# Results of a mixture-of-experts stage: stored by slot and gathered back, or scattered to their tokens and loaded plainly

## What is computed

```python
gate_weights = jax.nn.softmax(gate_logits, axis=-1)
topk_w, topk_idx = jax.lax.top_k(gate_weights, TOP_K)            # TOP_K = 2 of 8 experts
...
for e in range(NUM_EXPERTS):
    gate = jax.nn.silu(jnp.einsum('bsd,dh->bsh', x, W1[e]))
    val = jnp.einsum('bsd,dh->bsh', x, W3[e])
    y = jnp.einsum('bsh,hd->bsd', gate * val, W2[e])
    out = out + combine[..., e:e + 1] * y
```

## Time and profile before

| | |
|---|---|
| median of 3 runs | 1237.82 us (1235.93 to 1239.07) |
| the profiled execution, its own time | 1233.52 us |
| its span | 1231.8 us |
| mean granted clock of TensorE | 0.933 |
| PE busy | 1066.2 us, 87% |
| DVE busy | 586.4 us, 48% |
| ACT busy | 365.1 us, 30% |
| POOL busy | 238.2 us, 19% |
| layer 1, the loop over tiles | about 151 to 219.5 us |
| layer 1, from the last result to X | 219.5 to 246.3 us |
| layer 5, the loop over tiles | about 669 to 866.6 us |
| layer 5, from the last result to X | 866.6 to 892.0 us |

### The profile page before, as it was taken

One profiled execution on the slowest core, in us unless ns is written; L12 is line 12 of the kernel. 1 busy time (PEld: TensorE's weight loads), 2 busy tenths in 40 slices (PEclk: granted clock), 3 DMA queues, 4 the chain that ended last, 5 costly groups with the idle time before them and its releaser, 6 DMA issues.

```text
span 1231.8 us, 17738 instructions
## 1 busy us (share of the span) xinstructions
PE 1066.2 (87%) x6818; PEld 739.2 (60%) x6818; DVE 586.4 (48%) x1320; ACT 365.1 (30%) x675; POOL 238.2 (19%) x317
## 2 busy tenths in 40 slices
PE   5877999979999999978774999999179999879989
PEld 4665578736766666667563777777045555443457
DVE  6976322345434343445474221122256676248592
ACT  3642123232122222214220121121004544425570
POOL 4212332520000000003521110100541322011350
PEclk9986999979999999999986999999659999978999
DMA  9002022201011010055043112110230000020000
GB/s 274 15 2 94 18 84 79 86 26 35 22 30 35 18 35 5 10 202 219 2 167 107 31 31 81 35 30 14 77 142 2 1 2 1 1 69 1 0 9 26
DMA packets 36954, 65.31 MB, mean 53 GB/s; under 512 B 4456, under 2 KB 27848, under 8 KB 35464
## 3 DMA queue, kind: packets, MB, share of 16 engines
q1 hardware_dynamic: 26504, 47.91, 11.6%
q0 software_dynamic: 3744, 10.23, 3.1%
q10 hardware_dynamic: 6624, 6.03, 1.4%
HBM read 53.93 MB, written 10.22 MB: 52 GB/s over the span
## 4 chain that ended last, share of the span: by engine, by line
PE 73%; DVE 15%; issue 3%; DMA 3%; ACT 3%; POOL 2%; SPq 0%; DVEq 0%; ACTq 0%
PE bank L344 20%; PE bank L1132 12%; PE bank L1156 6%; PE bank L2020 5%; PE bank L1407 5%; PE bank L1415 2%; PE bank L2453 2%; PE bank L2064 2%; PE bank L2043 2%; PE bank L2035 2%; PE bank L1145 2%; PE bank L1392 1%; PE bank L1385 1%; PE bank L2075 1%; DVE big L1257 1%
## 5 line engine op out<-in xcount | busy, mean ns | idle before, releaser
L1132 PE MATMUL bank<-big 128*128 x552 | 153.8, 422 | 3.4 <-ACT big L1006 2.4
L344 PE MATMUL bank<-XNT,big 128*128 128x512 f32 x296 | 144.6, 641 | 4.5 <-DVE big L2202 2.8
L1132 PEld LDWEIGHTS bank<-big 128*128 128x128 f32 x552 | 96.4, 191 | 50.2 <-issue 11.9
L2020 PE MATMUL bank<-big,xs 32*128 32x512 f32 x256 | 85.7, 718 | 37.2 <-DVE xs L271 33.4
L265 POOL TENSOR_TENSOR rstd<-ve,half 128x1 f32<-128x1 f32 x64 | 38.8, 606 | 407.8 <-DVE ve L259 407.6
L1928 DVE TENSOR_REDUCE big<-bank 128x2 f32<-128x512 f32 x128 | 82.1, 685 | 49.9 <-PE bank L2020 49.8
L344 PEld LDWEIGHTS bank<-XNT,big 128*128 128x128 f32 x296 | 58.3, 204 | 73.0 <-issue 64.9
L1156 PE MATMUL bank<-big 128*128 (+1 forms) x368 | 87.2, 380 | 1.1 <-ACT big L1021 1.1
L1980 ACT ACTIVATE big<-bank 128x1024 f32<-128x1024 f32 x64 | 62.0, 1021 | 67.8 <-PE bank L2043 67.8
L950 DVE TENSOR_TENSOR big<-big,bank 128x704 f32<-128x704 f32 x23 | 20.4, 889 | 124.7 <-ACT big L1014 124.7
L344 PE MATMUL bank<-CTXT,big 128*128 128x512 f32 (+1 forms) x192 | 67.2, 494 | 10.7 <-DMA big<-wvT 10.7
(11 more groups left out here) (347 smaller groups left out, 1809.7 us busy)
## 6 DMA issues: line engine op xcount, KB each, us to landing
big<-m_gu SPq DMA_DIRECT2D x8, 1408.0 KB
big<-a_qkv SPq DMA_DIRECT2D x16, 384.0 KB, 3.6
big<-m_d SPq DMA_DIRECT2D x8, 768.0 KB
yg<-big ACTq DMA_DIRECT2D x46, 128.0 KB, 1.7
big<-m_gu SPq DMA_DIRECT2D x8, 352.0 KB
big<-a_o SPq DMA_DIRECT2D x16, 128.0 KB, 2.2
big<-p_gu SPq DMA_DIRECT2D x1, 2048.0 KB, 8.0
big<-m_d SPq DMA_DIRECT2D x8, 176.0 KB
```

The costliest lines, as they stand in the source:

```text
L344: ins = e.matmul(out, a, b, start=start and n == 0, stop=stop and n == len(pairs) - 1)
L1132: ins = e.matmul(out, xgT[s % 2][:, kb, :], WB[:, bass.ds(at[s] + (kb * 2 * F + c * chunk), chunk)], start=kb == 0, stop=kb == KB - 1)
L2020: e.matmul(bank[:, SBK + step % SBN, :], k.xs[t % 2][q, b * P:(b + 1) * P], cm[t % 2][q, 2 * jp:2 * jp + 2].rearrange("p j n -> p (j n)"), ...
```

## The change

The results no longer lie in `yg` by slot, but by token. `inv` now holds, for each slot, 128 + token + 1024*q, where q says whether it is the token's first or second expert; an empty slot still has 0. Rows 0 to 127 of `xn` and `yg` are there for the empty slots.

- **Stores of the normalised rows**: `xn` holds every row twice (at 128 + token and at 1152 + token), so that the same `inv` serves the fetch. SP stores each tile with a source that is read twice (256 rows of 1 KB instead of 128), and once tile 0 to rows 0 to 127.
- **In the loop**: ACT's store is gone. POOL scatters tile s to `yg` by an indirect DMA whose indices are `inv` (`deliver`), after its result is in SBUF and after the scatter of tile s-1 has landed. POOL's order is: fetches 0 to 3, then fetch s+4, deliver s, for every s.
- **At the end**: SP loads, for each token tile, both results in one plain DMA of 256 rows (`sp_last`), into four buffers by turns; the load of tile t waits until tile t-4 has been added. DVE's additions are the same.
- **SP's order**: the loads of layer 2 and layer 6 that stood ahead of the waits move ahead of the mixture's last loads (`sp_first`); the rest of SP's work stands behind them.
- `idx` and the DVE instruction that made it are gone.

```diff
-    idx, inv = U.take(2, NT, dt=I32), U.take(TILES, dt=I32)
+    inv = U.take(TILES, dt=I32)
...
-    xg, ya = ring[:, 0:RING], ring[:, RING:2 * RING]
+    xg, ya = ring[:, 0:RING], ring.rearrange("p (n q) d -> p n q d", q=2)
...
+    to_xn = xn_d[P:].rearrange("(c t p) d -> t p c d", p=P, t=NT)
+    from_yg = yg_d[P:].rearrange("(c t p) d -> t p c d", p=P, t=NT)
...
-            tell(e.dma_start(xn_d[t * P:(t + 1) * P, :], XN[:, t]), "xn_st", 16)
+            tell(e.dma_start(to_xn[t], bc(XN[:, t], 1, 2)), "xn_st", 16)
+            if t == 0:
+                tell(e.dma_start(xn_d[0:P], XN[:, 0]), "xn_st", 16)
+
+    def sp_last(e):
+        for q in range(YS):
+            after(e, f"y_st{q}", ends[f"y_st{q}"])
+        for t in range(NT):
+            if t >= 4:
+                e.wait_ge(k.x_tile, done0 + t - 3)
+            tell(e.dma_start(ya[:, t % 4], from_yg[t]), f"ga{t % 4}", 16)
...
-        after(e, "xn_st", 16 * NT)
-        for s in range(TILES):
+
+        def fetch(s):
             if s >= RING:
                 after(e, "xgt_ps", s - RING + 1)
             tell(e.indirect_dma_start(xg[:, s % RING], None, xn_d, bass.IndirectOffsetOnAxis(ap=inv[:, s:s + 1], axis=0)),
                  f"xg{s % RING}", 16)
-        for q in range(YS):
-            after(e, f"y_st{q}", ends[f"y_st{q}"])
-        for t in range(NT):
-            if t >= 2:
-                e.wait_ge(k.x_tile, done0 + t - 1)
-            for q in (0, 1):
-                tell(e.indirect_dma_start(ya[:, 2 * (t % 2) + q], None, yg_d,
-                                          bass.IndirectOffsetOnAxis(ap=idx[:, q, t:t + 1], axis=0)), f"ga{t % 2}", 16)
+
+        def deliver(s):
+            after(e, "y_sb", s + 1)
+            if s >= 1:
+                after(e, f"y_st{(s - 1) % YS}", 16 * ((s - 1) // YS + 1))
+            tell(e.indirect_dma_start(yg_d, bass.IndirectOffsetOnAxis(ap=inv[:, s:s + 1], axis=0), ys[s % YS], None),
+                 f"y_st{s % YS}", 16)
+
+        after(e, "inv", 1)
+        after(e, "xn_st", 16 * (NT + 1))
+        for s in range(RING):
+            fetch(s)
+        for s in range(TILES):
+            if s + RING < TILES:
+                fetch(s + RING)
+            deliver(s)
...
-            after(e, f"ga{p}", 32 * (t // 2 + 1))
-            ch.step(e.scalar_tensor_tensor(k.X[:, t], ya[:, 2 * p], wA[:, t:t + 1], k.X[:, t], ALU.mult, ALU.add))
+            after(e, f"ga{t % 4}", 16 * (t // 4 + 1))
+            ch.step(e.scalar_tensor_tensor(k.X[:, t], ya[:, t % 4, 0], wA[:, t:t + 1], k.X[:, t], ALU.mult, ALU.add))
...
-        def store(s):
-            after(e, "y_sb", s + 1)
-            tell(e.dma_start(yg_d[s * P:(s + 1) * P, :], ys[s % YS]), f"y_st{s % YS}", 16)
...
-            if s >= 1 + LAG:
-                store(s - 1 - LAG)
-        for s in range(TILES - 1, TILES):
-            store(s)
...
                 if who + "_first" in s:
                     s[who + "_first"](e)
+                if n > 0 and who + "_last" in stages[n - 1]:
+                    stages[n - 1][who + "_last"](e)
```

More of the change, by code:

```diff
@@ L163, in shared @@
     k.row_no = k.sb("row_no", [P, P])
-    k.token_no = k.sb("token_no", [P, NT])
+    k.token_no = k.sb("token_no", [P, 2, NT])
     k.zeros = k.sb("zeros", [P, P])
@@ L201, in pool @@
                allow_small_or_imprecise_dtypes=True).then_inc(k.const, 1)
-        e.iota(k.token_no[:, :], pattern=[[P, NT]], base=0, channel_multiplier=1,
+        e.iota(k.token_no[:, :, :], pattern=[[T, 2], [P, NT]], base=P, channel_multiplier=1,
                allow_small_or_imprecise_dtypes=True).then_inc(k.const, 1)
@@ L730 @@
             "xg0", "xg1", "xg2", "xg3", "xgt_ps", "xgt_sb", "gu_ps", "hs", "h_sb", "ht_ps", "ht_act", "ht_dve",
-            "y_ps", "y_sb", "y_st0", "y_st1", "ga0", "ga1", "sh_ps", "sh_s", "sh_u", "sh_h", "shy_ps", "shy")
+            "y_ps", "y_sb", "y_st0", "y_st1", "ga0", "ga1", "ga2", "ga3", "sh_ps", "sh_s", "sh_u", "sh_h", "shy_ps", "shy")
 def experts(k, l, F, chunk, row, base, shared_expert, prefix):
@@ L789, in experts @@
     S, start = k.moe, dict(k.moe_at)
-    ends = dict(gate_ld=16 * (1 + 4 * shared_expert), wts=16 * 2 * E, xn_st=16 * NT, lg_ps=NT, mx=1, ex=1, mk=1, cnt=1,
+    ends = dict(gate_ld=16 * (1 + 4 * shared_expert), wts=16 * 2 * E, xn_st=16 * (NT + 1), lg_ps=NT, mx=1, ex=1, mk=1, cnt=1,
                 hot=2, inv_ps=1, inv_sb=1, inv_t=1, inv=1, eid=1, xgt_ps=TILES, xgt_sb=TILES, gu_ps=TILES, hs=TILES, h_sb=TILES,
-                ht_ps=TILES, ht_act=TILES, ht_dve=TILES * (NB > 4), y_ps=TILES, y_sb=TILES, ga0=16 * NT, ga1=16 * NT,
+                ht_ps=TILES, ht_act=TILES, ht_dve=TILES * (NB > 4), y_ps=TILES, y_sb=TILES, ga0=32, ga1=32, ga2=32, ga3=32,
                 sh_ps=6, sh_s=6, sh_u=6, sh_h=6, shy_ps=NT, shy=NT)
@@ L839, in pool @@
                 tell(e.tensor_tensor(both, both, sg[n % 2][0:FB[n % 3]], ALU.mult), "sh_h")
-        after(e, "inv", 1)
-        after(e, "xn_st", 16 * NT)
-        for s in range(TILES):
+        def fetch(s):
             if s >= RING:
@@ L912, in dve @@
         ch.step(e.tensor_tensor(pos[:, 1], sumd, pos[:, 0], ALU.subtract))
-        ch.mark(e.tensor_scalar(idx, pos, -1.0, None, ALU.add))
         ch.step(e.tensor_scalar(pt, pos, 1.0 / P, -0.5 - 0.5 / P, ALU.mult, ALU.add))
@@ L918, in dve @@
         ch.step(e.tensor_tensor(slot, bc(pt, 3, TILES), bc(bc(k.slot_no[:, :], 1, NT), 1, 2), ALU.is_equal))
-        ch.step(e.tensor_tensor(slot, slot, bc(bc(k.token_no[:, :], 2, TILES), 1, 2), ALU.mult))
+        ch.step(e.tensor_tensor(slot, slot, bc(k.token_no[:, :, :], 3, TILES), ALU.mult))
         for q in (0, 1):
@@ L973, in dve @@
         for t in range(NT):
-            p = t % 2
-            after(e, f"ga{p}", 32 * (t // 2 + 1))
-            ch.step(e.scalar_tensor_tensor(k.X[:, t], ya[:, 2 * p], wA[:, t:t + 1], k.X[:, t], ALU.mult, ALU.add))
-            e.scalar_tensor_tensor(k.X[:, t], ya[:, 2 * p + 1], wB[:, t:t + 1], k.X[:, t], ALU.mult, ALU.add)\
+            after(e, f"ga{t % 4}", 16 * (t // 4 + 1))
+            ch.step(e.scalar_tensor_tensor(k.X[:, t], ya[:, t % 4, 0], wA[:, t:t + 1], k.X[:, t], ALU.mult, ALU.add))
+            e.scalar_tensor_tensor(k.X[:, t], ya[:, t % 4, 1], wB[:, t:t + 1], k.X[:, t], ALU.mult, ALU.add)\
                 .then_inc(k.x_tile, 1)
@@ L1174, in pe @@
                 down(s - 2)
-    return dict(sp=sp, pool=pool, dve=dve, act=act, pe=pe)
+    return dict(sp=sp, sp_last=sp_last, pool=pool, dve=dve, act=act, pe=pe)
 def attention_wide(k, l):
@@ L1212, in qk_at, with load, load_o, sp_first @@
         return 4 * h - 2 * min(h, FIRST)
-    def sp(e):
[L1215 to L1225, removed]
+    def load(e, h):
+        e.dma_start(w3[h % FIRST], g["a2_qkv"][h:h + 1].rearrange("h p c k f -> p (h c) k f"))\
+            .then_inc(wsem[h % FIRST], 16)
+    def load_o(e, h):
+        e.dma_start(wo[h % 2], g["a2_o"][h:h + 1].rearrange("h p d -> p (h d)")).then_inc(osem[h % 2], 16)
+    def sp_first(e):
+        for h in range(FIRST):
+            load(e, h)
+        load_o(e, 0)
+        load_o(e, 1)
+    def sp(e):
         for h in range(H):
@@ L1231, in sp @@
                     e.wait_ge(S["v_ps"], h - FIRST + 1)
-                load(h + FIRST)
+                load(e, h + FIRST)
             if 1 <= h < H - 1:
                 e.wait_ge(S["wo_ps"], 4 * h)
-                load_o(h + 1)
+                load_o(e, h + 1)
     def pool(e):
@@ L1433, in pe @@
         out_proj(H - 1, last=True)
-    return dict(sp=sp, pool=pool, dve=dve, act=act, pe=pe, pe_first=pe_first, act_first=act_first)
+    return dict(sp=sp, sp_first=sp_first, pool=pool, dve=dve, act=act, pe=pe, pe_first=pe_first, act_first=act_first)
 class Stages:
@@ L2109, in pe @@
         sort(NT - 1)
-    return dict(sp=sp, pool=pool, dve=dve, act=act, pe=pe)
+    return dict(sp_first=sp_first, pool=pool, dve=dve, act=act, pe=pe)
 def peer_mlp(k, l):
@@ L2556, in program @@
     with ExitStack() as ctx:
-        dram = dict(dram, xn=nc.dram_tensor("xn", (T, D), F32, kind="Internal").ap(),
-                    yg=nc.dram_tensor("yg", (TILES * P, D), F32, kind="Internal").ap(),
+        dram = dict(dram, xn=nc.dram_tensor("xn", (2 * T + P, D), F32, kind="Internal").ap(),
+                    yg=nc.dram_tensor("yg", (2 * T + P, D), F32, kind="Internal").ap(),
                     xd=nc.dram_tensor("xd", (T, D), F32, kind="Internal").ap(), out=out)
```

## The result

The changed kernel takes 1231.99 us in the median of 5 runs (1230.18 to 1233.35), the kernel before 1237.82 (5 runs, 1235.48 to 1239.07) on the same chip. The ratio is 0.9954, with a 95% interval of 0.9936 to 0.9973. Two later comparisons on other chips gave 1.0005 (0.9984 to 1.0027) and 0.9983 (0.9967 to 0.9998); they are under "experiments". The mean of the three ratios comes to some 2.4 us less, and only the second interval takes in "no change". The profiled execution took 1230.32 us with a span of 1228.5, where the one before took 1233.52 and 1231.8.

The account below looks back on a forecast made before the run. PE (73% of the span) was taken to bound the kernel, except where it waits for transfers. For the profiled execution 1233.5 + 9.8 - 3.4 - 10.3 = 1229.6; for the median 1237.8 - 3.9 = 1233.9 us, range 1224 to 1249.

Parts of the forecast that it names:

- Layer 5's end: From layer 5's last result copy to complete X, uncovered on PE: scatter, loads and additions replace store and gathers, -10.3 us.
- Layer 1's loop: Layer 1's mixture rounds: fetches queued behind scatters on POOL lengthen the loop by 9.8 us.
- The cycle of the fetch: Layer 1's loop: turn, result copy, POOL's scatter descriptors, then fetch to landing; 6.1 us per two rounds instead of 5.62.
- the second cycle: Layer 1's loop: each scatter waits for the one before to land; round is scatter + 0.27, 2.97 us at 2.7.
- the two cycles meet: Layer 1's loop: the fetch chain and the scatter-to-scatter chain were said to meet at a scatter of 2.9 us.
- Slow fetches: Layer 1's loop: fetches of tiles with 30 or more empty slots, all reading row 0, add 5.4 us.
- the seven: Layer 1 fetches for tiles 9, 11, 14, 17, 20, 21 and 22, taking 3.2 to 4.0 us, 25.0 together.
- Layer 2's norm: After layer 1: X is ready before PE finishes keys and values, covered by 7 us, so the norm saves 3.4 us.
- What costs nothing: Doubled row stores are covered in layers 1 and 5; the `idx` instruction and ACT issues save 0.1 us at most.
- Rival 1: Fetches aren't held up in layer 1's loop; layer 1 gains 3.4 and layer 5 10.3: 1224.1 us, chance 0.12.
- Rival 2: Scatters' own chain decides layer 1's loop, scatters being slower: no gain at 3.1 us, 1246.3 at 3.5; chance 0.28.
- Rival 3: Empty slots' writes to row 0 cost 3 us, at four loop tiles and layer 5's end: about +4, 1242; chance 0.08.

Follow-up runs that it names:

- the two halves: The change in layer 5 alone (10.6 us less than the kernel before) and in layer 1 alone (10.5 us more), timed on one chip.
- e1: The change in layer 5 only, layer 1 storing and gathering as in the kernel before: 1222.01 us, ratio 0.992 to the kernel before.
- e5: The whole changed kernel again, on another chip: 1237.35 us, ratio 1.0005 to the kernel before.
- e10: The whole changed kernel once more, on a further chip: 1235.04 us, ratio 0.9983 to the kernel before.
- e6: Changed kernel, separate dump rows for even and odd tiles' empty slots, scatter waiting only for the one two before: 1228.76 us, ratio 0.993 to the kernel before.
- e4: Changed kernel with eight fetched-row buffers in layer 1 instead of four: 1233.31 us, ratio 1.0011 to the kernel before.
- e3: Changed kernel, empty slot on partition p reading and writing row p instead of row 0: 1232.45 us, ratio 1.0006 to the kernel before.
- e8: The change in layer 5 alone, empty slots going to dump rows of their own: 1228.76 us, ratio 0.9939 to the kernel before.
- e11: Second run of: changed kernel, own dump rows, no wait for the scatter before, eight row buffers in layer 1. 1229.44 us, ratio 0.9947 to the kernel before.
- e7: Changed kernel, own dump rows, no wait for the scatter before, eight row buffers in layer 1: 1230.66 us, ratio 0.9951 to the kernel before.

## Why the prediction was right, and where it wasn't

The forecast was 1233.9 and 1231.99 was measured; for the profiled execution it was 1229.6 against 1230.32. The agreement is partly luck: a term that was too small by 4 to 5 us met 4 us that lie in code the change doesn't touch. By the rows that are the change's, the profile shows +0.9, not -3.9; the two halves sum to -0.1; the medians of the three comparisons mean -2.4.

- **Layer 5's end, -10.3: right.** e1 measured -10.6. From the last copy to X it took 14.3 us for the 15.1 of the working. The 0.7 are the scatter's: to one row it took 3.13, not 3.8 (2.40 and 0.74 more, for 2.7 and 1.1). From the first load to X it was 10.9, for 11.0. In e1, e5 and e10 the scatter was as short, but the loads and additions took 11.7 to 11.8, so that copy to X was 15.1 to 15.2: there two small errors cancel.
- **Layer 1's loop, +9.8: too little by 4.6** (+14.4; in the other executions +13.9 to +15.4). The cycle of the fetch is as predicted: the turns wait for the DMA, a fetch starts 1.30 after a scatter, and where this cycle stands alone (e6) two rounds take 6.2 us for 6.1. One step failed by its size, the price of the second cycle, "its round is scatter + 0.27, 2.97 us at 2.7". The 0.27 came from POOL waking after DVE's addition. After its own scatter has landed POOL needs 0.77. With the scatter's 2.43 that is 3.20, as long as a scatter of 2.93 would have made it by the 0.27, just beyond 2.9, where "the two cycles meet". By the prediction's own formula, 17 x (3.20 - 2.81) + 3.6, the loop would have grown by 10.2, so this step is only a small part of the 4.6. For the rest the prediction has no term. Two transfers of tiles without empty slots were 0.9 and 1.5 too long (3.32 for 2.43, 4.29 for 2.8), each with an `instruction` packet in it. And PE was at half clock twice, 1.1 and 1.0 us (below). These four overlap with other waits, so they can't be added exactly. e4 has the fetch's cycle taken out and e6 the scatters'; their loops grow by 12.2 and 7.3, and both hold some of these four.
- **Slow fetches, 5.4 of it: the cause was right.** With rows of their own (e3) the loop lost 4.7. But this takes away slow fetches and slow scatters at once. And tile 11 doesn't belong to the seven: its 3.2 us, put down to 30 empty slots, had an `instruction` packet in it (at 171.5), and with the change the same fetch took 2.57.
- **Not foreseen:** the full clock is lost inside the loop. The fetch of tile 13 took 4.29, PE waited 1.65 of it, and the next round ran in part at 0.50. Windows of the changed kernel, at the loop's start and there:
```profile
151.00:153.00 2.00, 2.00 (x7) 2.00 (x8) 0.00 (x0) 0.00 (x0) 0.41 (x1) 0.50 0.17 35
192.00:194.00 2.00, 0.35 (x4) 0.10 (x3) 0.34 (x1) 0.59 (x2) 1.47 (x2) 1.00 0.21 70
194.00:196.00 2.00, 2.00 (x10) 1.89 (x11) 0.42 (x1) 0.37 (x1) 0.00 (x0) 0.80 0.27 66
196.00:198.00 2.00, 2.00 (x10) 1.89 (x9) 0.00 (x0) 0.32 (x1) 1.69 (x2) 0.50 0.18 66
198.00:200.00 2.00, 2.00 (x11) 1.76 (x11) 0.76 (x2) 0.74 (x2) 0.27 (x1) 0.85 0.21 66
```
  The round from the turn at 193.93 to that at 197.78 takes 3.85 with nobody waiting, 1.0 more than at full clock. In the first row PE is at 0.50 before any result has been scattered: the first two rounds took 6.5 us, for 5.4 in before. This isn't the cycles' doing, and not a fixed part of the kernel either: in e5 the same two rounds took 5.4.
- **Layer 2's norm, -3.4: right,** 3.5 measured. X was covered by 4.9 us and not 7: the last scatter started at 239.27, when the working had it landed at 238.9; but the keys and values were 2.9 us later than foreseen, too.
- **What costs nothing: right.** In layer 5 the doubled stores were over by 668, 7 us before the first fetch:
```profile
662.00:665.00 3.00, 0.09 (x1) 0.00 (x0) 2.42 (x14) 0.00 (x0) 0.00 (x0) 0.50 1.09 384
665.00:668.00 3.00, 0.00 (x0) 0.00 (x0) 2.76 (x10) 0.00 (x0) 0.00 (x0) 0.50 0.69 242
```
- **The rivals.** Rival 1 (fetches aren't held up) fell: PE's turns waited for their fetch 15 times. Rival 2 (the scatters' chain decides) was half true: its chain is as long as with a scatter of 2.93 in the prediction's sum, for another reason than the one given. Taking its wait away is worth 2.5 us of the loop (e6 against e3). The reason given was that a scatter to DRAM takes longer than a fetch from it. It took 2.40, the fetches 2.8. The Trainium skill ("DMA: Bandwidth & Descriptors", Anatomy of one DMA) would have had it slower for the write's receipt; that ranking isn't borne out here. The Trainium skill's fit in the same section gives an estimate of 2.3 us for 128 KB, and this is near the 2.40 measured. Rival 3 (writes to one row dear) had the effect right and its size wrong: 0.74, less than the 1.1 charged.

## What to carry to other kernels

Judge such a change at each place where it is made: the same edit was worth -10.6 us where nothing covered the wait, and +10.5 where a loop of 2.8 us a round had its slack in POOL's queue. That slack also hid every transfer that happened to be long; without it each one counts. A DMA behind another on one queue ties two cycles together; add up each from landing to the next issue, and take the wake-up time from a row in which that engine waits for that kind of DMA. And cut the spans at common events before crediting a difference of a few us: 4.2 us, more than the whole net gain of 3.3 between the profiles, were in code that the change leaves alone.

## What the runs showed of the hardware

- POOL begins its next indirect DMA 0.77 us after the landing of its own last one, SP a plain one 0.02 after such a landing (880.26), DVE an instruction 0.1 after (199.30 to 199.39). POOL after a plain store's landing: 0.26, and 0.24 after DVE's copy ahead of the same two waits (199.83 to 200.07 in e4). What the 0.77 is made of stays open.
- An indirect store of 128 rows of 1 KB lands in 2.40 us, in 3.14 when all go to one row of DRAM (e8 and e1).
- Eight indirect transfers of 128 rows took 4.0 to 4.8 us in the loops' chains, and during each a packet of the `instruction` queue ran. Cause inferred, not tried.
- After the idle time at layer 5's end PE stayed at 0.50 until about 31 us after X in nine profiled executions and until 42 to 52 us in four (e11, e6, e7, e8), with the same code from there on. Layers 6 and 7 took 336.9 to 340.5 us in the nine, and 341.7, 344.0, 344.1 and 348.1 in the four. What decides it stays open.
